# A reordered first layer with stand-in products on TensorE in its first beat

## The reference, cut to what matters

```python
x = L0_attn_x
xn = _layernorm(x, axis=-1)
x = x + _L0_attn_ref(xn, ...) + _L0_ffn_ref(xn, ...)
...
# _L0_attn_ref
h = rmsnorm(x, norm1_w)
x = x + _gla(h, wq, wk, wv, gk_w1, gk_w2, gk_b, wg, gnorm_w, wo)
h2 = rmsnorm(x, ffn_norm_w)
ffn = jax.nn.silu(h2 @ w_gate) * (h2 @ w_up) @ w_down
return x + ffn
# _gla, one chunk
qe = qc * jnp.exp(b)
A = jnp.einsum('bhik,bhjk->bhij', qe, kc * jnp.exp(-b)) * mask
o = jnp.einsum('bhck,bhkv->bhcv', qe, S) + jnp.einsum('bhij,bhjv->bhiv', A, vc)
S = jnp.exp(bl[:, :, 0, :])[..., None] * S + jnp.einsum('bhck,bhcv->bhkv', kc * jnp.exp(bl - b), vc)
# _L0_ffn_ref
scores = jax.nn.softmax(jnp.abs(logits).astype(jnp.float32), axis=-1)
_, idx = jax.lax.top_k(scores + extra_bias[None, :], TOPK)
```

## Time and profile before

| | us |
|---|---|
| median of three runs | 2991.1 |
| the profiled execution | 3019.2 |
| its span, first to last instruction | 3017.4 |
| end of the first layer in that span | 789.4 |
| PE busy (17318 products) | 2684.2, 89% |
| DVE busy | 2343.3, 78% |
| ACT busy | 2077.5, 69% |
| POOL busy | 1974.2, 65% |
| mean granted clock of PE | 0.943 |

### The profile page before, as it was taken

The page is one execution under the profiler, slowest core; times in us unless marked ns, Lnnn a source line. Parts: engine busy times, 40 slices in busy tenths (PEclk is TensorE's granted clock), DMA queues, the critical chain, the costliest instruction groups (busy, mean ns, idle before and its releaser), DMA issues.

```text
span 3017.4 us, 58651 instructions
## 1 busy us (share of the span) xinstructions
PE 2684.2 (89%) x17318; PEld 2117.3 (70%) x17318; DVE 2343.3 (78%) x5975; ACT 2077.5 (69%) x4671; POOL 1974.2 (65%) x1697
## 2 busy tenths in 40 slices
PE   5899999987199786479799999999999999999997
PEld 3566666655189564467588787887878878778786
DVE  5566666664377497468699999998989999999896
ACT  3454444433355465355699999998999999999996
POOL 3222222225334215555599999998999999999998
PEclk8799999998699897689899999999999999999999
DMA  5565654546666453547787776756666666666563
GB/s 134 147 201 184 195 189 167 169 151 230 183 189 199 164 178 131 175 128 236 214 252 238 229 236 192 236 198 219 222 200 222 201 215 213 207 220 208 190 223 113
DMA packets 322100, 588.35 MB, mean 195 GB/s; under 512 B 48784, under 2 KB 141232, under 8 KB 321296
## 3 DMA queue, kind: packets, MB, share of 16 engines
q1 hardware_dynamic: 307440, 545.07, 57.8%
q0 software_dynamic: 14352, 39.54, 3.6%
HBM read 464.45 MB, written 124.17 MB: 195 GB/s over the span
## 4 chain that ended last, share of the span: by engine, by line
POOL 35%; issue 10%; ACT 3%; DVE 1%; PE 1%; DMA 1%; POOLq 1%; SPq 0%; DVEq 0%; ACTq 0%
POOL mm L2735 8%; POOL y L2748 7%; POOL yz L2752 7%; POOL y L2762 6%; POOL y_lo L2741 6%; ACT mt L2665 1%; DVE cv L2818 1%; DMA wi<-ssm_wi_split 1%; POOLq L2411 1%; ACT mt L2685 0%; ACT ys L2679 0%; ACT L2700 0%; POOL first L2777 0%; DVE bank L2889 0%; PE bank L64 0%
## 5 line engine op out<-in xcount | busy, mean ns | idle before, releaser
L2735 POOL TENSOR_TENSOR mm<-mt,cb 128x512 f32<-128x512 f32 x384 | 492.8, 1307 | 56.4 <-ACT mt L2685 53.9
L2665 ACT ACTIVATE mt<-a_wide,a_tok 128x128 f32<-128x128 f32 x1536 | 487.2, 389 | 3.7 <-POOL mm L2735 2.9
L2818 DVE SCALAR_TENSOR_TENSOR cv<-bank,taps,cv 128x509 f32<-128x509 f32 (+2 forms) x576 | 429.5, 746 | 13.6
L64 PE MATMUL bank<-f,wi 128*128 128x512 f32 x768 | 322.1, 419 | 14.8 <-DMA wi<-ssm_wi_split 14.8
L66 PE MATMUL bank<-f,wi 128*128 128x512 f32 x768 | 305.5, 398 | 0.0
L65 PE MATMUL bank<-f,wi 128*128 128x512 f32 x768 | 305.4, 398 | 0.0
L2752 POOL TENSOR_TENSOR yz<-y,zs 128x512 f32<-128x512 f32 x192 | 248.8, 1296 | 15.1
L2741 POOL TENSOR_TENSOR y_lo<-yz,y_hi 128x512 fp32r<-128x512 f32 x192 | 246.8, 1285 | 8.1 <-ACT y_hi L2690 6.1
L2748 POOL TENSOR_TENSOR y<-t 128x512 f32<-128x512 f32 x192 | 246.8, 1285 | 0.0
L965 POOL TENSOR_TENSOR l_s_out<-l_s_raw,l_s_out 128x768 fp32r<-128x768 f32 x33 | 61.2, 1854 | 277.8 <-ACT l_s_out L811 277.8
L2558 PE MATMUL bank<-mm,x_tok 128*64 128x128 f32 x3072 | 226.8, 283 | 13.5 <-POOL mm L2735 13.4
(11 more groups left out here) (479 smaller groups left out, 8075.4 us busy)
## 6 DMA issues: line engine op xcount, KB each, us to landing
wi<-ssm_wi_split SPq DMA_DIRECT2D x192, 512.0 KB
a_wide<-a_scratch SPq DMA_DIRECT2D x192, 512.0 KB
l_fw<-ffn_split SPq DMA_DIRECT2D x72, 768.0 KB
ea<-ea_scratch SPq DMA_DIRECT2D x384, 128.0 KB
wo<-ssm_wo_split SPq DMA_DIRECT2D x192, 256.0 KB, 3.7
sorted_scratch<-ex_zeros SPq DMA_DIRECT2D x96, 130.5 KB
ssm_wi_split<-l_s_out SPq DMA_DIRECT2D x24, 512.0 KB
x_all<-sorted_scratch SPq DMA_DIRECT2D x94, 130.5 KB
```

The lines of the kernel that those rows point to most:

```text
L64: pe.matmul(out, wh, xh, start=first, stop=False)
L2665: i = act.activation(mt[:, h, chunk(j)], a_wide[:, g % R, h, chunk(j)], ACT.Relu, bias=a_tok[:, s * NJ + j, 2 * t + h:2 * t + h + 1], scal ...
L2735: pl.tensor_tensor(mm[:, :, ts], mt[:, :, ts], cb[:, js, :].rearrange("p j t -> p (j t)") .unsqueeze(1).broadcast_to([P, 2, TS // 2]), ALU ...
L2818: dve.scalar_tensor_tensor(cv[:, a:TS], bank[:, X, 0:TS - a], taps[:, t, k:k + 1], cv[:, a:TS], ALU.mult, ALU.add).then_inc(ph["tap"], 1)
```

## The change

Seven edits, all in `layer0`:

- `slots`: beat 0 has splits in steps 0, 2, 4, 6 (before also 8), beat 1 in 0, 1, 2, 3, 6 (before 0, 2, 4, 6, 7), the last three beats also in step 7.
- DVE: `gate_product` stands behind `hidden_low`; `first_norm(k + 1)` in step 2 (before 0); `choose` in step 5 (before 1); the placing's five parts in steps 1, 2, 2, 3, 3 (before 1 to 5).
- POOL: the low parts of steps 1 and 2 stand ahead of the last two masked queries, the sum `base` behind them.
- PE: `ranks` in step 1 of beat 7, behind that step's `gate_up` (before in step 0, ahead of `output_gate`); `outputs` waits for the copied ranks in place of `output_gate`.
- ACT: the copy of the ranks in step 1.
- SP: three of four rows read back in step 6 of beat 7 in place of its end.
- PE: in beat 0 `keep_busy(n)` issues n products of 128x512 of weights already there, into a bank that nothing reads, ahead of and behind the other work of each step: 114 in all.

```diff
-        slots = [(-1, 4)] + [(0, t) for t in (0, 2, 4, 6, 8)] + [(1, t) for t in (0, 2, 4, 6, 7)]
-        slots += [(k, t) for k in range(2, G) for t in (0, 2, 4, 6)]
+        slots = [(-1, 4)] + [(0, t) for t in (0, 2, 4, 6)] + [(1, t) for t in (0, 1, 2, 3, 6)]
+        slots += [(k, t) for k in range(2, G - 3) for t in (0, 2, 4, 6)]
+        slots += [(k, t) for k in range(G - 3, G) for t in (0, 2, 4, 6, 7)]
...
+                        if k == G - 1 and t == 6:
+                            for i in range(1, RX):
+                                rows_back(i)
...
                     if k == G - 1:
-                        for i in range(1, RX + 1):
-                            rows_back(i)
+                        rows_back(RX)
...
                     if j == 0:
                         done(pe, "sgate", c)
+                        if c == G - 1:
+                            done(pe, "ranked", 0, 2)
...
                     done(pe, "pick", G - 1)
-                    done(pe, "r2_ln", G - 2)
+                    done(pe, "sgate", G - 1)
...
-                    else:
-                        done(pe, "ranked", 0, 2)
...
+                def keep_busy(n):
+
+                    for _ in range(n):
+                        pe.matmul(bank[:, 6, :], w_hi[:, 0, 0:P], w_hi[:, 1, 0:TS], start=True, stop=True)
...
                         if core:
                             scores(k, j)
+                        if k == 0:
+                            keep_busy(6)
                         if has(f):
                             gate_up(f, t)
                         if has(k) and t == 0:
-                            if k == G - 1:
-                                ranks()
                             output_gate(k)
                             turn(k)
+                        if k == G - 1 and t == 1:
+                            ranks()
                         if core:
                             updates(k, j)
+                        if k == 0:
+                            keep_busy(4)
...
                         if core:
                             outputs(k, j)
+                        if k == 0 and t >= HEADS:
+                            keep_busy(6)
...
                     low(split_of(k, 0))
                     if has(k):
                         for n in range(4, 6):
                             masked(k, n)
+                    low(split_of(k, 1))
                     low(split_of(k, 2))
                     if has(k):
                         for n in range(6, NC0):
                             masked(k, n)
...
+                    low(split_of(k, 3))
                     low(split_of(k, 4))
                     if has(k + 2):
                         x_half(k + 2)
-                    for t in (6, 7, 8):
+                    for t in range(5, NT):
                         low(split_of(k, t))
...
-                        if has(k) and t == 0:
-                            gate_product(k)
...
                         if has(f):
                             hidden_low(f, t)
+                        if has(k) and t == 0:
+                            gate_product(k)
                         if core:
                             advance(k, 2 * j + 1)
-                        if has(k + 1) and t == 0:
+                        if has(k + 1) and t == 2:
                             first_norm(k + 1)
-                        if 0 <= k < G - 1 and t == 1:
+                        if 0 <= k < G - 1 and t == HEADS:
                             choose(k)
...
-                        if k == G - 1 and 1 <= t <= PLACE_PARTS:
-                            next(placing, None)
+                        if k == G - 1:
+                            for _ in range({1: 1, 2: 2, 3: 2}.get(t, 0)):
+                                next(placing, None)
```

More of the change, by code:

```diff
@@ L902, in _ @@
                             act.preload_act_table_set("natural_log_exp_and_others")
-                        if has(f):
-                            hidden_high(f, t)
-                        if k == G - 1 and t == 0:
+                        if k == G - 1 and t == 1:
                             done(act, "ranks", 0)
@@ L909, in _ @@
                                 act.activation(ranked[:, i * TS:i * TS + NG * E0], bank[:, i, 0:NG * E0], ACT.Copy).then_inc(ph["ranked"], 1)
+                        if has(f):
+                            hidden_high(f, t)
                         if has(k) and t == 0:
@@ L984, in _ @@
                             masked(k, n)
+                    low(split_of(k, 0))
+                    if has(k):
+                        for n in range(4, 6):
+                            masked(k, n)
+                    low(split_of(k, 1))
+                    low(split_of(k, 2))
+                    if has(k):
+                        for n in range(6, NC0):
+                            masked(k, n)
                     if has(k + 1):
@@ L988, in _ @@
                         pl.tensor_tensor(base[:, (k + 1) % 3], x[(k + 1) % 2], xn[:, (k + 1) % 3], ALU.add).then_inc(ph["base"], 1)
-                    low(split_of(k, 0))
-                    if has(k):
-                        for n in range(4, 6):
-                            masked(k, n)
-                    low(split_of(k, 2))
-                    if has(k):
-                        for n in range(6, NC0):
-                            masked(k, n)
+                    low(split_of(k, 3))
                     low(split_of(k, 4))
```

## The result

The changed kernel takes 2955.49 us (median of 4 runs, 2949.76 to 2965.99) against 2993.12 for the kernel before in the same rounds: ratio 0.9877, interval 0.9843 to 0.9912. That is 37.6 us faster. The forecast was 2944 with a range of 2918 to 2974, 47 us faster; the time lies in the range and the direction is right, but a fifth of the saving is missing. The profiled execution has a span of 2964.2 us and a time of 2965.99.

A forecast was written before the change was run, and what follows sets the result against it. TensorE was taken to bound beats 0 to 6 of the first layer, the scatter's start its end. Terms -5.0 + 34.9 + 17.0 = 46.9 us saved from 3019.2 give 2972, less 28.1 for the median 2944; range 2918 to 2974.

The forecast's parts named there:

- beats 0 and 1: First layer's first two beats: 5.0 us lost together, although beat 0 alone gave 7.5.
- beats 2 to 6: TensorE's wait before the first state update shrinks and the half clock goes with it: 34.9 us saved.
- from beat 7's start to the scatter: Ranks later and placing packed into steps 1 to 3 of beat 7: scatter starts 17.0 us earlier.
- Beat 0: Stand-in products keep full clock: 9.0 us saved up to the last output, token rows start near 95.3 instead of 100.62.
- the last 48 lie on the path: Beat 0's tail: ScalarE's and VectorE's work for the attention's output product would be ready 5.6 us before TensorE gets through.
- Beat 1: Splits in neighbouring steps make ScalarE's copies wait on a 15.0 us refill chain; beat grows from 87.7 to some 98.
- The rival that the refills hide: Beat 1: later writes land early enough not to hold ScalarE; 20 us more saved, 2924; chance 0.14.
- The rival that the clock falls all the same: Beats 2 to 6: half clock stays despite the shorter wait; costs 21.5 us, 2966; chance 0.13.
- The rival that they don't hold the clock: Beat 0: stand-in products leave TensorE at 1.2 GHz; 27 us lost, 2971; chance 0.15.
- The slower rival: Every beat: a write landing 20 us after issue holds ScalarE's tanh; 10 us a beat, 3004; chance 0.05.
- The prediction's sign of being wrong: Behind the first layer: a later layer that doesn't keep its 2228 us would show the prediction wrong.
- The rule on the clock: Beat 0's attention steps: 33.85 of 43.00 us busy yet clock 0.50, against the skill's rule that the gate follows busyness.

The follow-up runs named there:

- e9: Changed kernel with the placing's five parts one to a step again (steps 1 to 5 of beat 7); layer's end 750.19 us against 754.61.
- e5: Changed kernel with the whole old table of slots and all 114 stand-in (keep_busy) products; 2936.63 us in one run.
- e7: Changed kernel with all old slots and stand-in products only in steps 0 to 4 of beat 0 (50 of 114); median 2931.63 us, ratio to before 0.9799.
- e13: Changed kernel again, unchanged, for a second profile; layer's end 750.62 us against 754.61 in the first.
- e2: Changed kernel with the old slots in beats 0 and 1 only, later slots as changed; median 2939.68 us, ratio to before 0.9834.
- e1: Changed kernel without its 114 stand-in products; median 2952.17 us, ratio to before 0.9866.
- e3: Changed kernel with the next group's first norm back in step 0; beats 2 to 6 take 415.75 us against 395.91.
- e8: Changed kernel with all old slots and no stand-in products; median 2936.23 us, ratio to before 0.9809.
- e6: Kernel before with the 114 stand-in products added and nothing else; 2992.81 us in one run against a median of 2990.18 for before.
- e10: Kernel before, unchanged, for a second profile; layer's end 784.17 us against 786.77, the rest 2200.9 against 2230.6.
- e4: As e3, with 13 stand-in products ahead of the first update in beats 2 to 6 to fill the wait; these beats take 412.02 us.
- e12: Changed kernel with all old slots and only the six stand-in products behind the scores in steps 0 to 4 of beat 0; median 2930.05 us, ratio 0.9792.

## Why the prediction was right, and where it was short

The mechanisms were those forecast; most of the sizes were too favourable. From profile to profile:

| term | forecast saved | measured |
|---|---|---|
| beats 0 and 1 | -5.0 | -8.0 (189.26 to 197.27) |
| beats 2 to 6 | 34.9 | 29.3 |
| from beat 7's start to the scatter | 17.0 | 13.05 |
| scatter | 0 | -2.15 |
| the layer | 46.9 | 32.2 |
| behind the layer | 0 | 21.0 |

**Beat 0, mis-sized by 3.5.** The token rows were to start near 95.3 and started at 98.82, 1.8 earlier than before instead of 5.3. The 21.1 from the last output to the token rows came out to the tenth (77.74 to 98.82). What failed is the part ahead of it, which was to save 9.0 and saved 5.4 (the last stretch of outputs ended at 83.2 before and at 77.8 after). The first update came at 53.08 instead of 51.0: the front was 0.5 late before its clock fell and lost 1.3 in the 24 products from 36.81 to 41.02, which ran in part at half clock. In e9, which is the same code up to there and whose front kept its clock, the forecast comes out (timelines of PE, after and e9):

```profile
53.08 0.70 PE L565 MATMUL bank<-l_v,l_klt 64*128 64x256 f32 x4
```

```profile
51.06 0.70 PE L565 MATMUL bank<-l_v,l_klt 64*128 64x256 f32 x4
```

The other 1.5 are in the steps: four took 27.26, 6.6 each and one wait of 0.80, instead of 6.3 each, since six and four stand-ins took 1.59 and 1.03 and not 1.4 and 0.9. The step was right that the last 48 lie on the path: without the stand-ins behind the attention steps beat 1 starts 3.0 earlier (97.55 in e5, 94.60 in e7), less than the 5.6 named, since the output product then runs at half clock.

**Beat 1, right.** Forecast: copies 15.0 apart, ScalarE idle for 8 to 11 us ahead of three of them, a beat of 98. Measured: 13.43 to 15.07, 8.83 to 9.53, 97.49 (95.06 in e13). One reason given beside it failed: the front of beat 1 did not keep its clock (0.50 from 104.7 to 108.1), and the first gate product came 3.7 earlier (117.33 before, 113.67 after), not 7.5. The rival that the refills hide is refuted by these rows, and e2 prices the crowding at 17.25 (with the fifth split of beat 0 put back beside it).

**Beats 2 to 6, mis-sized by 5.6.** The idle time of TensorE fell from 20.88 to 9.70, by 11.2 and not by 13.4 (14.4 + 0.5 - 1.5); the splits in step 7 cost 1.8 and 2.2 beside the 78.2 of beat 3, not 0.75 each, for ScalarE waits up to 5.72 for the write. Without them these beats are 1.7 shorter (e5); with them beat 5 varies, from 78.7 in e1 and e9 to 80.1. The wait that was to be left at 0.55 in each beat is 3.9 in 10 waits, 0.8 a beat. The clock gave 18.1 (busy 404.30 to 386.21) and not 21.5. Rounding of the mean clock was not the fault: the stretches at 0.50 in beats 2 to 6 of the kernel before (216.0 to 229.7, 304.8 to 308.2, 386.7 to 390.1, 468.6 to 482.3 and 557.3 to 567.6) add up to 44.4, half of which is 22.2. What failed is the step from half clock to half the time lost: TensorE stood still for 2.2 of the 44.4, and not all work takes twice as long. Two stretches of outputs follow each other 0.99 apart at 0.50 (kernel before, beat 0) and 0.61 apart at 1.00 (after):

```profile
73.20 0.69 PE L574 MATMUL bank<-l_qe,l_state 128*128 128x64 f32 x2
...
74.19 0.69 PE L574 MATMUL bank<-l_qe,l_state 128*128 128x64 f32 x2
```

```profile
69.93 0.43 PE L579 MATMUL bank<-l_qe,l_state 128*128 128x64 f32 x2
...
70.54 0.43 PE L579 MATMUL bank<-l_qe,l_state 128*128 128x64 f32 x2
```

The 18.1 are 41% of the 44.4. The rival that the clock falls all the same is refuted at 1.00 (e13 has a single fall, from 517.8 to 521.2, behind a wait of 1.36 in the front of beat 6). The reason given for this term held, with one limit: e3 shows that waits of 2.79 and 2.87 can pass without a fall.

**Beat 7 and the scatter, mis-sized by 4.** The first update came 29.2 after the start of the beat instead of 26.3, and the packed placing took 32.55 from there instead of 31.5. The 2.9 are waits and half clock in the front of the beat, behind the split in step 7 of beat 6, which the forecast charged to beats 5 and 6 alone. In the timeline of PE after:

```profile
597.75 1.12 PE L616 MATMUL bank<-l_kl,tab 16*128 16x512 f32 x2 [1.09 <-ACT l_kl L862]
...
600.13 2.04 PE L720 MATMUL bank<-l_xo,tab 128*128 128x512 f32 x2 [1.26 <-POOL l_xo L992]
...
622.39 0.70 PE L565 MATMUL bank<-l_v,l_klt 64*128 64x256 f32 x4
```

The second of them runs at half clock (2.04; 1.10 in the kernel before). In e9 the same two waits (0.96 and 1.26) bring no fall and the first update comes 27.6 after the beat's start, so some 1.6 of the 2.9 are the clock. With the old slots the first wait is gone and the second 0.42: in e5 the first update comes 26.3 after the beat's start (573.37 to 599.68), as forecast, and the scatter 58.6 after it, within 1 us of the 57.8 forecast (74.81 - 17.0).

**Stand-ins.** The rival that they don't hold the clock is refuted (1.00 from 47 to 95). But the forecast counted the clock they hold as a gain, and that was the wrong question. They are worth nothing with the new slots (e1). With the old slots all 114 are worth up to 5 us (e8 to e5, by single profiles; the times don't show it). Those in the attention steps alone are worth 4.6 by the medians (e8 to e7); the layer's end says 9.2, but e8's profiled execution was its slowest run and e7's its fastest. Without the new order they cost 4.1 at beat 1's start (e6).

**The slower rival** asked for a write that lands 20 us after its issue. The landing in the rows after is 4.3 (132.73 to 137.03), and no wait for the masked queries is among TensorE's in beats 2 to 6.

**The sum against the median.** The forecast kept the 28.1 by which the profiled execution of before stood over its median. e10 shows that this was right and where it lay: 29.7 behind the layer, by chance. The prediction's sign of being wrong, a later layer that doesn't keep its 2228, came true by the letter (2209.6 behind the scatter for 2230.6), but the kernel before itself took 2200.9 there in e10, so the sign says nothing about the change. Counted from the profile after, 53.2 were saved, of which 21.0 are this chance; from medians 37.6; the layer alone gives 32.2 (33.5 between the second profiles). What is between 32.2 and 37.6 is within the spread of the runs.

**The rule on the clock.** The prediction puts a stretch with 33.85 of 43.00 us busy and a clock of 0.50 beside the rule of the Trainium skill ("TensorE: Matmul & The Clock Gate", What's actually happening) that the gate follows how busy the engine has been lately. The runs agree with it in part: e4's filled waits brought no fall, and the same waits unfilled (e3) brought three in five. Other rows leave it open: e1 repeats the prediction's row (34.71 of 45.00 at 0.54), e12 has 26.23 of 30.00 at 1.00, and falls also followed waits of about 0.5. Shares of busy time at the two clocks can't be compared directly, since a record is longer at half clock (0.69 instead of 0.43 for the outputs above). No number of the sum hung on it.

## What to carry to other kernels

Where one buffer is refilled in a chain (copy, low part, fetch, write), take the chain's length from the trace before the slots are set closer than that: here 13.4 to 15.1 us against steps of 8.7 to 9.4 (beat 1 of e2) cost 17 us, a third of what the rest of the change brought. Price stand-in products as work on the path: here they paid where they fill the waits of the attention steps (e7, 4.6 by the medians) and not behind these, and in the old order, with a longer wait left, they cost more than they gave (e6). When the profiled execution stands off the median, take a second profile and find the stretch in which it does before the sum is made against it.

## What was not expected of the hardware

- Whether the clock falls at a short stand-still differs between kernels, and between executions of the same code (in beat 7's front after but not in e9): behind 2.79 to 2.87 us in three of five beats (e3), behind 3.43 to 3.47 in all five, in both profiles of before, with the same beats long (87.7 and 87.8, 82.7 and 82.6, 86.7 and 86.3 for beats 2, 3 and 5). A fall also followed waits of only 0.51 us (e3, product at 326.62, clock 0.54 from 328 to 330) and 0.46 (e4, product at 576.67). So it was a fact of one trace that waits of up to 0.8 brought no fall, as the prediction read it.
- The same 64 scatters of the first layer took 94.9 to 99.7 us, and 97.5 and 94.9 in two executions of one kernel.
- One stretch of the second layer's experts took 92.9 or 69.8 us in two executions of one kernel; the cause is open.
